# Expert update of batches 0 to 4 from high and low parts stacked in two fp32r matmuls

## The reference

```python
x_diff = x[:, None] - select_mean_diff[None, :, None]       # x = layernorm(h), 8 experts
x_diff = x_diff / norm(x_diff)
score = ((select_weight . x_diff) ** 2).sum(-1)
gate = sigmoid(imp_slope * (score - imp_center))
best, idx = gate.max(experts), gate.argmax(experts)
mod_x = lora_update[idx] . (x - debias_w[idx])              # 8 values a token
y = (1 - best) * x + best * (bias_w[idx] + lora_degen[idx] . mod_x)
```

## Time and profile before

| | |
|---|---|
| median of 3 runs | 817.11 us (816.69 to 817.26) |
| profiled execution: its own time | 815.06 us |
| its span | 813.3 us |
| granted PE clock over the span | 0.996 of full speed |
| update product, 16 tiles in all | 10 tiles are those of batches 0 to 4 |

### The profile page before, as it was taken

The page is one execution under the profiler, slowest core; times in us unless marked ns, Lnnn a source line. Parts: engine busy times, 40 slices in busy tenths (PEclk is TensorE's granted clock), DMA queues, the critical chain, the costliest instruction groups (busy, mean ns, idle before and its releaser), DMA issues.

```text
span 813.3 us, 19702 instructions
## 1 busy us (share of the span) xinstructions
PE 747.9 (92%) x6970; PEld 678.4 (83%) x6970; DVE 569.0 (70%) x1600; ACT 455.8 (56%) x1250; POOL 445.2 (55%) x660
## 2 busy tenths in 40 slices
PE   0366778999999999999999999999999999999997
PEld 0166667899999999999999999999999999988974
DVE  7999758787766666665566655665665777788777
ACT  6734426666665656555575665555756556455442
POOL 1497836754444747444456474444656655665632
PEclk9999999999999999999999999999999999999999
DMA  9023360100010102000001020000010000000002
GB/s 213 1 60 69 81 233 27 39 1 0 0 40 2 53 1 79 0 0 0 0 1 52 2 79 0 0 0 0 14 40 1 2 1 27 26 26 0 26 1 104
DMA packets 30503, 26.47 MB, mean 33 GB/s; under 512 B 22446, under 2 KB 22830, under 8 KB 30198
## 3 DMA queue, kind: packets, MB, share of 16 engines
q1 hardware_dynamic: 30310, 25.77, 11.2%
q10 hardware_dynamic: 144, 0.07, 0.0%
HBM read 17.44 MB, written 8.39 MB: 32 GB/s over the span
## 4 chain that ended last, share of the span: by engine, by line
PE 77%; DVE 8%; POOL 7%; ACT 4%; issue 3%; DMA 1%; DVEq 0%; SPq 0%; POOLq 0%; ACTq 0%
PE bank_quad L1324 17%; PE bank_quad L1326 16%; PE bank_quad L1325 16%; PE bank_pair L1326 4%; PE bank_pair L1324 4%; PE bank_pair L1325 4%; POOL w_lo L433 2%; PE bank_quad L1336 2%; PE bank_quad L1425 2%; PE bank L1501 1%; PE bank_pair L1491 1%; PE bank L1505 1%; PE bank_pair L1501 1%; DVE bank_pair L974 1%; POOL kq_lo L511 1%
## 5 line engine op out<-in xcount | busy, mean ns | idle before, releaser
L1324 PE MATMUL bank_quad<-xt_hi,w_hi 128*128 (+1 forms) x768 | 217.0, 282 | 1.4 <-POOL w_lo L433 0.8
L1326 PE MATMUL bank_quad<-xt_lo,w_hi 128*128 (+1 forms) x768 | 214.7, 280 | 0.0
L1325 PE MATMUL bank_quad<-xt_hi,w_lo 128*128 (+1 forms) x768 | 214.5, 279 | 0.0
L1062 DVE TENSOR_TENSOR kq<-bank_quad,cst 128x512 f32<-128x512 f32 (+1 forms) x96 | 57.8, 602 | 134.8 <-ACT swap L725 101.2
L506 POOL TENSOR_TENSOR swap<-swap,cst 128x512 f32<-128x512 f32 (+1 forms) x96 | 105.7, 1103 | 82.2 <-ACT swap L725 77.2
L1324 PEld LDWEIGHTS bank_quad<-xt_hi,w_hi 128*128 128x128 f32 x768 | 144.5, 188 | 3.9 <-issue 1.7
L1326 PEld LDWEIGHTS bank_quad<-xt_lo,w_hi 128*128 128x128 f32 x768 | 144.5, 188 | 0.0
L1325 PEld LDWEIGHTS bank_quad<-xt_hi,w_lo 128*128 128x128 f32 x768 | 144.4, 188 | 0.0
L357 POOL TENSOR_TENSOR spare<-cst 1x1 f32<-1x1 f32 x85 | 17.5, 206 | 204.3 <-DVE rinv L1206 140.0
L768 ACT ACTIVATE sm<-sm,mx 128x128 f32<-128x128 f32 (+1 forms) x256 | 113.5, 445 | 20.6 <-DVE mx L1194 20.6
L724 ACT ACTIVATE swap<-bank_quad 64x512 f32<-64x512 f32 (+1 forms) x96 | 50.2, 523 | 118.6 <-PE bank_quad L1326 115.7
(11 more groups left out here) (313 smaller groups left out, 1861.7 us busy)
## 6 DMA issues: line engine op xcount, KB each, us to landing
mixed<-st SPq DMA_DIRECT2D x32, 128.0 KB, 2.0
out<-x SPq DMA_DIRECT2D x16, 256.0 KB, 2.0
raw<-in_w_qkv SPq DMA_DIRECT2D x8, 384.0 KB, 3.7
raw<-in_w_o SPq DMA_DIRECT2D x10, 256.0 KB, 2.6
x<-mixed SPq DMA_DIRECT2D x2, 1280.0 KB, 10.4
norm_mem<-in_w_qkv SPq DMA_DIRECT2D x6, 384.0 KB, 3.7
x<-mixed SPq DMA_DIRECT2D x3, 512.0 KB, 4.6
norm_mem<-in_w_o SPq DMA_DIRECT2D x6, 256.0 KB, 2.8
```

The costliest lines, as they stand in the source:

```text
L1062: v.tensor_tensor(view(kq), src, table(cosT), ALU.mult).then_inc(kq_cos, 1)
L1324: mmul(dst, lh, rh, start=start and k == 0, stop=False, skip_group_check=True)
L1325: mmul(dst, ll, rh, start=False, stop=False, skip_group_check=True)
L1326: last = mmul(dst, lh, rl, start=False, stop=stop and k == n - 1, skip_group_check=True)
```

## The change

The update products of batches 0 to 4 take fp32r operands of 128 rows. Weights: the 72 rows of `dw` as high parts and their low parts are laid in two tables of 128 x 512 (`upd_w`, in memory of `xt_l` that is free by then). Tokens: the 72 rows as high parts and low parts are laid in two tables of 128 x 256 (`upd_m`). A tile is then two fp32r matmuls in one accumulation; they cover high x high, high x low and low x high (the one-hot rows have no low part). Batches 5 to 7 keep the fp32 matmul.

New work: DVE zeroes 32 rows of the weights' tables (`pad_update`, step 0 of group 3) and subtracts three low parts (`split_update`, step 1); ACT rounds the weights (`update_weights`, step 1). For each batch ACT makes four copies out of bank 7 (`mt_stack`) where it made one, and DVE one subtraction (`mt_rest`), between heads 1 and 2 of the next step's masked scores. PE waits for `mt_lo` as well.

```diff
+            def update_weights():
+                act.wait_ge(gate_in, 80)
+                act.wait_ge(upd_pad, 1)
+                nc.scalar.activation(upd_w[0][0:MC], dw[:], ACT.Copy)
+                nc.scalar.activation(upd_w[1][0:64], dw[0:64], ACT.Copy).then_inc(upd_hi, 1)
+            def mt_stack(bb):
+                act.wait_ge(mt_ready, bb + 1)
+                nc.scalar.activation(upd_m[0][0:MC], banks[7][0:MC, 0:S], ACT.Copy)
+                nc.scalar.activation(upd_m[0][96:128], banks[7][0:32, 0:S], ACT.Copy)
+                nc.scalar.activation(upd_m[1][96:128], banks[7][32:64, 0:S], ACT.Copy)
+                nc.scalar.activation(upd_m[1][64:MC], banks[7][64:MC, 0:S], ACT.Copy).then_inc(mt_done, 1)
...
+                if g == NG - 1 and at == 1:
+                    update_weights()
                 round_attn(i)
                 round_v(i + 1)
                 if needs_ffn(g, at):
-                    mt_evac(b - 2)
+                    mt_stack(b - 2)
...
                     if j == 1 and not first:
                         attn_rest(i - 1, 1)
+                        if update is not None:
+                            mt_rest(update)
...
+            def pad_update():
+                old = xt_h[64:96, 0].rearrange("p k s -> p (k s)").bitcast(F32)
+                v.tensor_tensor(xt_l[64:96, 0].rearrange("p k s -> p (k s)"), old, old, ALU.subtract).then_inc(upd_pad, 1)
+            def split_update():
+                dve.wait_ge(upd_hi, 1)
+                for k, (dst, src) in ((0, (slice(96, 128), slice(0, 32))), (1, (slice(96, 128), slice(32, 64))),
+                                      (1, (slice(64, MC), slice(64, MC)))):
+                    last = v.tensor_tensor(upd_w[k][dst], dw[src], upd_w[0][src].bitcast(F32), ALU.subtract)
+                last.then_inc(upd_lo, 1)
+            def mt_rest(bb):
+                dve.wait_ge(mt_done, bb + 1)
+                v.tensor_tensor(upd_m[1][0:64], banks[7][0:64, 0:S], upd_m[0][0:64].bitcast(F32), ALU.subtract).then_inc(mt_lo, 1)
...
                 add_output(i - 1, (b - 1) if at else NB - 1, (1,))
+                if g == NG - 1 and at == 0:
+                    pad_update()
+                if g == NG - 1 and at == 1:
+                    split_update()
...
+            def stacked_tile(t, bank):
+                rows = slice(t * P, (t + 1) * P)
+                mmul(banks[bank][:], upd_m[0][:, rows], upd_w[0], start=True, stop=False)
+                mmul(banks[bank][:], upd_m[1][:, rows], upd_w[1], start=False, stop=True).then_inc(d_ready, 1)
...
-                        update_product(b - 3)
+                        if at == 3:
+                            pe.wait_ge(upd_lo, 1)
+                        stacked_product(b - 3)
...
             pe.wait_ge(mt_done, NB - 3)
+            pe.wait_ge(mt_lo, NB - 3)
             transpose_probs(last)
...
-            update_tile(mt[:, 0:P], 2)
+            stacked_tile(0, 2)
...
-            update_tile(mt[:, P:2 * P], 7)
+            stacked_tile(1, 7)
```

More of the change, by code:

```diff
@@ L249, in tower @@
         xt_l = sb("xt_lo", [P, NB, KC, S], F32R)
+        upd_w = [xt_l[:, 0, 2 * k:2 * k + 2, :].rearrange("p k s -> p (k s)") for k in range(2)]
+        upd_m = [xt_l[:, 1, k, :] for k in range(2)]
         woh = sb("wo_hi", [P, QH, D], F32R)
@@ L343, in tower @@
         xn_scaled, xn_added, x7_added = sem("xn_scaled"), sem("xn_added"), sem("last_xn_added")
+        upd_pad, upd_hi, upd_lo, mt_lo = sem("upd_pad"), sem("upd_hi_done"), sem("upd_lo_done"), sem("mt_lo_done")
         mt_ready, mt_done, d_ready, out_ready, stored = (
@@ L1186, in attn_rest, with masked_scores @@
                                 ALU.subtract).then_inc(ot_lo, 1)
-            def masked_scores(i, first=False, with_v=True):
+            def masked_scores(i, first=False, with_v=True, update=None):
                 for j in range(QH):
@@ L1212, in probs_rest @@
                                     ALU.subtract).then_inc(pt_lo, 1)
+            def pad_update():
[10 more added lines that the diff above has]
+                v.tensor_tensor(upd_m[1][0:64], banks[7][0:64, 0:S], upd_m[0][0:64].bitcast(F32), ALU.subtract).then_inc(mt_lo, 1)
             def step(g, b, at):
                 i = b + 8 * g
-                masked_scores(i)
+                masked_scores(i, update=b - 3 if needs_finish(g, at) else None)
                 if needs_norm1(g, at):
@@ L1271, in _ @@
             last = NG * NB - 1
-            masked_scores(last, with_v=False)
+            masked_scores(last, with_v=False, update=NB - 4)
             reciprocals(last, (0,))
@@ L1443, in update_tile, with stacked_product @@
                 mmul(banks[bank][:], rows, dw[:], start=True, stop=True).then_inc(d_ready, 1)
+            def stacked_tile(t, bank):
+                rows = slice(t * P, (t + 1) * P)
+                mmul(banks[bank][:], upd_m[0][:, rows], upd_w[0], start=True, stop=False)
+                mmul(banks[bank][:], upd_m[1][:, rows], upd_w[1], start=False, stop=True).then_inc(d_ready, 1)
+            def stacked_product(bb):
+                pe.wait_ge(mt_done, bb + 1)
+                pe.wait_ge(mt_lo, bb + 1)
+                for t in range(TT):
+                    stacked_tile(t, 5 + t)
             def update_product(bb):
```

## The result

The change made the kernel slower: 819.81 us median of 6 runs (819.59 to 821.28) against 817.18 of the kernel before measured beside it (816.2 to 818.0), a ratio of 1.0037 with an interval of 1.0027 to 1.0047. That is 2.6 us more. The forecast was 0.7 us more (817.8) and a range up to 819.4, so the loss is outside it. The profiled execution took 819.66, its span 817.9.

What follows compares the result with a forecast made beforehand. TensorE and VectorE were taken as nearly level, VectorE setting TensorE's time in step 2. Split +1.67, steps 3 to 6 -1.0, tail +0.34 -0.32 gave +0.7 us: 817.8 us, range 816.0 to 819.4 (8 times in 10).

Steps and rivals of the forecast that it cites:

- VectorE sets TensorE's time: Last group: TensorE waits for VectorE's results; slack 0.13 and 0.70 us in step 4, 0.05 us hand-over in step 2.
- The split, +1.67: Step 2: three VectorE subtractions at 0.60 each, less 0.13 us of waiting, are paid in full: 1.67 us.
- Steps 3 to 6, -1.0: Four steps with an update product: the transposes start 0.31 earlier, take 0.06 more, gaining 0.25 each, 1.0 us in all.
- The term for `mt_rest`, 0.34: Steps 3 to 6: the new VectorE subtraction delays masked scores and normed tokens by 0.34 us.
- the hand-over: From VectorE's end to TensorE's start, ahead of product and transposes: 0.05 us, as read in step 2.
- ScalarE and the padding, nothing: ScalarE's four copies hide in a 1.50 us wait; step 0's padding, even blocked up to 1.3 us, costs nothing.
- The tail, +0.02: Batch 4's update: `mt_rest` delays probabilities by 0.34 us, the shorter second tile gains 0.32, so 0.02 more.
- Rival 1: Steps 3 to 6: VectorE's added work is free, TensorE keeps 0.9 a step, 3.4 in all; 815.1 us, chance 0.10.
- the 0.79: Steps 3 to 6, TensorE alone: four fp32r matmuls take 1.03 in place of 1.82 us, gaining 0.79 a step.
- Rival 2: Split: each of three subtractions meets a GpSimd instruction, 1.27 in place of 0.60, 2.0 more; 819.8 us, chance 0.10.
- Rival 3: Steps 3 to 6: normed tokens come 0.6 late, not 0.34, and the whole gain is lost; 818.8 us, chance 0.15.
- Adding the 2.05 between the profiled execution and the median: Whole kernel: the median is 2.05 us above the profiled execution; added to the profiled forecast of 815.8 to give 817.8.

Runs made afterwards that it cites:

- e8: Changed kernel with padding and split spread over steps 0 and 1, `mt_rest` after normed tokens, TensorE's transposes then product between two Q heads: 813.14 us, ratio 0.9953.
- e1: Changed kernel with only the weights' preparation kept; update products and the old token copy as in the kernel before: 819.48 us, ratio 1.0035.
- e6: Changed kernel with the split's three subtractions writing 72 rows from partition 0 and reading from partition 0: 819.68 us, ratio 1.0029.
- e3: Changed kernel without VectorE's subtraction `mt_rest` and the two waits for it: 817.49 us, ratio 1.0011.
- e7: Changed kernel with the tail's second update tile again as one fp32 matmul of 72 rows: 820.01 us, ratio 1.0032.
- e2: Changed kernel without the weights' preparation (`update_weights`, `pad_update`, `split_update`) and TensorE's wait for it: 816.39 us, ratio 0.9993.
- e9: Kernel before with only TensorE's new order: transposes of normed tokens, then fp32 product, between two heads of the first Q half: 816.57 us, ratio 0.9997.

## Why the prediction was wrong

**VectorE sets TensorE's time: right.** The waits stand where they were forecast, ahead of the transposes of step 2, ahead of the product, and ahead of the transposes behind it. e8 shows the reverse: with VectorE's results early, TensorE's own 0.80 a step comes out.

**The split, +1.67: mechanism right, size wrong.** Measured 2.10 to 2.11 (e1 alone: 24.88 against 22.78). The step that failed is "I take the free price: 3x0.60=1.80". The time does go by columns (8 rows cost what 32 do), but 0.60 is a spacing between instructions that overlap, and these three change their start partition and don't. e6 shows 1.68 once they all start at 0. This is 0.43 of the miss.

**Steps 3 to 6, -1.0: mechanism right, size wrong.** Measured -0.63 against the profiled kernel before (98.61 to 97.98), -0.75 against e1 (98.73). The term for `mt_rest`, 0.34, was right (e3: 0.34 a step), and so was the product (0.34 and three times 0.23 forecast; 0.30, 0.24, 0.23 from start to start). What failed is the hand-over: 0.05 us from VectorE's end to TensorE's start, read at one place in step 2, was 0.13 ahead of the transposes, with `mt_rest` and without it (e3). That is 0.08 a step, some 0.3 of the miss. Ahead of the product it was 0.24, but this costs nothing more, since the tokens come last. Which of the waits in a row there makes the 0.24 wasn't tried.

**ScalarE and the padding, nothing: right.** The padding was blocked by GpSimd for 1.1 us, forecast at up to 1.3, and it stayed hidden.

**The tail, +0.02: wrong.** Both terms were right (+0.37 for +0.34, -0.39 for -0.32). What was missing is what a faster tile sets off: VectorE's product moved under GpSimd's additions, +0.35. The rule for it stood in the prediction, but I asked it only of the split. e7 shows gain and loss cancel. The stretch behind VectorE's last instruction, the stores, was 0.46 longer too (2.49 before, 2.95 after). I don't count that to the change: it is 2.45 to 2.50 in six of the eleven traces and 2.89 to 2.98 in five, and e2, whose tail is the changed kernel's instruction for instruction, has 2.49. The five with the long stretch are the five executions with the lowest mean granted clock (0.986 to 0.989, the others 0.990 to 0.996). Why there are two lengths is open.

**The rivals.** Rival 1 (VectorE's added work is free) is out by e3. Its 0.9 a step for TensorE was too high as well: with no wait in front the first fp32r matmul of the product still takes 0.32 in e8 (704.20 to 704.52), so the 0.79 holds either way; and 4x0.9-0.1 is 3.5, not 3.4. Rival 2 (the split blocked by GpSimd) gave the right time, 819.8, by the wrong cause: nothing blocks the split where the change puts it, and e6 has it at 1.68. Rival 3 (the gain eaten whole) had the direction right, for a quarter to a third of the gain. Put together: 0.7 forecast, 0.43 for the quadrants, 0.3 for the hand-over and 0.35 for the lock make 1.8, and the trace without the stores shows 2.34-0.46=1.88. The times show 2.63 (by the ratio's interval 2.2 to 3.8), so at least 0.3 us of the loss is not located; the stores and the front, which differ by more than that between the traces, are where it could lie. What the first two misses have in common: I took the shortest spacing and the shortest hand-over seen, and each of them could only grow.

Adding the 2.05 between the profiled execution and the median came out right: the profiled execution of the kernel after is only 0.15 under its median. As far as these traces tell, it lies in the front. The mark of step 1 is at 639.39 there and at 640.32 to 641.98 in the other ten traces, mostly later where the granted clock from 50 to 150 us was lower. The clock is not all of it: e9, with the same 0.97 and 0.97, has its mark 0.93 later.

## What to carry to other kernels

When two engines are nearly level, a cheaper instruction on the one gains only what the other's results allow: look at when the results come and put work that is ready ahead of the wait, as e8 does with the same matmuls and subtractions. Before a small preparation goes into a gap of VectorE, look at what GpSimd does in that gap, at whether the step has time to spare, and at the partitions where the operands start. And when something comes 0.4 us earlier, ask what it then runs beside.

## What the runs showed of the hardware

- VectorE instructions that start in another quadrant (32 partitions) than their predecessor took 0.70 from start to start at 512 columns, for 8 rows as for 32; those that all start at partition 0 took 0.60, for 72 rows as for 128.
- ScalarE shows something like it: the four copies of `mt_stack` start 0.39 apart, while the copy to partition 0 starts 0.27 behind its predecessor (700.82 to 701.09). This was read, not tested.
- Three VectorE subtractions beside GpSimd's work took 4.61 in place of 2.1, and GpSimd lost over 1 us as well: both sides pay for the lock.
- A fp32r matmul of 128 rows and 512 columns costs 0.23 to 0.24 from start to start, one in fp32 of 72 rows 0.86 (0.96 behind fp32r work). The first fp32r matmul of 512 columns costs 0.32 behind fp32 transposes with no wait (e8). Where all is ready, two stacked tiles are 0.80 us shorter than two in fp32.
